# One core of an attention and feed-forward kernel: the last batch's residual chain placed otherwise among the plain units

## The reference, cut to what matters

```python
x = x + xattn(layernorm(x), ctx, mask, ...)         # 16 heads; the result is scaled and layer-normed
h = layernorm(x)
h = fwht(h * SU_ug) / 64                            # Walsh-Hadamard transform over 512 columns
h = silu(h @ W_gate.T * s_gate) * (h @ W_up.T * s_up)   # 2048 columns
h = fwht(h * SU_dp) / 64
x = x + h @ W_down.T * s_down
```

## Time and profile before

| what | value |
|---|---|
| median of 3 runs | 1454.08 us (1452.18 to 1454.42) |
| the profiled execution, its own time | 1452.16 us |
| its span, first to last instruction | 1450.3 us |
| mean granted TensorE clock | 0.997 of full speed |
| TensorE busy with products | 1407.1 us (97%) |
| VectorE busy | 1107.4 us (76%) |
| ScalarE busy | 814.2 us (56%) |
| GpSimd busy | 88.8 us (6%) |
| eight plain units, first product to the last before the pairs | 929.87 to about 1030 us |

### The profile page before, as it was taken

The page is one execution under the profiler, slowest core; times in us unless marked ns, Lnnn a source line. Parts: engine busy times, 40 slices in busy tenths (PEclk is TensorE's granted clock), DMA queues, the critical chain, the costliest instruction groups (busy, mean ns, idle before and its releaser), DMA issues. The chain is left out here.

```text
span 1450.3 us, 25099 instructions
## 1 busy us (share of the span) xinstructions
PE 1407.1 (97%) x10344; PEld 954.1 (66%) x10344; DVE 1107.4 (76%) x1655; ACT 814.2 (56%) x1018; POOL 88.8 (6%) x128
## 2 busy tenths in 40 slices
PE   7999999999999999999999999998999999999997
PEld 6787333788333688333689333586788888888886
DVE  6953999885999895899885899887866565656654
ACT  5345999535999635899635899534533333333330
POOL 1000000101000100000100000110010010000100
PEclk9999999999999999999999999999999999999999
DMA  8453000536100425000424500362345554454435
GB/s 275 151 185 153 9 10 10 177 104 218 52 10 10 147 98 190 21 17 10 141 74 175 241 17 10 97 240 86 146 147 208 189 182 149 163 208 176 174 145 174
DMA packets 54785, 180.91 MB, mean 125 GB/s; under 512 B 11168, under 2 KB 25760, under 8 KB 42384
## 3 DMA queue, kind: packets, MB, share of 16 engines
q1 hardware_dynamic: 39696, 116.08, 22.2%
q0 software_dynamic: 14976, 63.23, 12.7%
HBM read 111.97 MB, written 67.31 MB: 124 GB/s over the span
## 5 line engine op out<-in xcount | busy, mean ns | idle before, releaser
L960 ACT ACTIVATE cx_probs<-cx_sc,proj_mbias 128x1024 f32<-128x1024 f32 (+1 forms) x416 | 442.7, 1113 | 48.2 <-PE cx_sc L1234 24.6
L1103 DVE TENSOR_SCALAR cx_probs<-cx_probs 128x1024 f32<-128x1024 f32 (+1 forms) x416 | 269.8, 685 | 50.8 <-ACT cx_probs L960 49.0
L1069 DVE TENSOR_TENSOR cx_padd<-cx_probs,cx_probs 128x1024 f32<-128x1024 f32 x192 | 234.0, 1219 | 0.9
L1234 PEld LDWEIGHTS cx_sc<-cx_q,cx_kt 32*128 32x128 f32 (+1 forms) x2496 | 103.7, 180 | 192.2 <-ACT cx_probs L960 172.5
L1257 PE MATMUL cx_acc<-cx_probs,cx_vt 128*32 128x512 f32 (+1 forms) x1664 | 218.1, 596 | 3.8 <-DVE cx_probs L1103 3.8
L1234 PE MATMUL cx_sc<-cx_q,cx_kt 32*128 32x512 f32 (+1 forms) x2496 | 206.5, 425 | 10.2 <-ACT cx_probs L960 7.1
L140 PE MATMUL ff_yp<-hand_wds,ff_held 128*128 128x512 f32 x624 | 143.7, 389 | 0.1
L1702 DVE TENSOR_TENSOR ff_x<-ff_yp,ff_x 128x512 f32<-128x512 f32 x128 | 85.4, 688 | 68.5 <-PE ff_yp L140 57.6
L140 PEld LDWEIGHTS ff_yp<-hand_wds,ff_held 128*128 128x128 f32 x624 | 117.0, 188 | 24.8 <-DVE ff_kept L1765 0.5
L1269 PE MATMUL cx_tot<-cx_padd,cx_ones 128*32 128x256 f32 x1536 | 120.8, 390 | 0.0
L902 ACT ACTIVATE cx_kt<-cx_sc,proj_bk 128x256 fp32r<-128x256 f32 (+1 forms) x96 | 44.5, 478 | 74.6 <-PE cx_sc L140 74.2
(11 more groups left out here) (294 smaller groups left out, 2057.7 us busy)
## 6 DMA issues: line engine op xcount, KB each, us to landing
ff_x<-scr_x SPq DMA_DIRECT2D x32, 1024.0 KB, 5.0
scr_x<-ff_x SPq DMA_DIRECT2D x28, 1024.0 KB, 4.7
proj_raw<-in_ctxT SPq DMA_DIRECT2D x20, 512.0 KB, 5.7
hand_wds<-scr_wd POOLq DMA_DIRECT2D x7, 1024.0 KB, 9.9
scr_q<-cx_q SPq DMA_DIRECT2D x3, 2048.0 KB, 6.5
cx_wo<-scr_wo POOLq DMA_DIRECT2D x3, 2048.0 KB, 13.7
scr_xs<-cx_xs POOLq DMA_DIRECT2D x3, 2048.0 KB, 7.9
cx_q<-scr_q SPq DMA_DIRECT2D x3, 1536.0 KB, 10.8
```

What stands on the lines that cost most here:

```text
L960: nc.scalar.activation(prob(N)[0:r], bank_of(n)[0:r], ACT.Exp, bias=mbias[0:r, b, t:t + 1], scale=SCALE).then_inc(exp_done, 1)
L1069: nc.vector.tensor_tensor(padd[z][(g * QP + j) % 2][:], prob(2 * i + z)[:], prob(2 * i + 2 + z)[:], ALU.add).then_inc(added[z], 1)
L1103: nc.vector.tensor_scalar(prob(N)[0:r], prob(N)[0:r], LOW, HIGH, ALU.max, ALU.min).then_inc(clip_done, 1)
L1234: last = nc.tensor.matmul(bank_of(2 * i + h // 2)[0:r, h % 2], kt[own, z, c, t * P:t * P + r], q[own, y, c], start=n == 0, stop=n == 2)
```

## The change

Five edits. ScalarE does the second root (k = 1) behind the silu of unit 4 instead of at the end of unit 3, and VectorE does `normed`, and a turned sum with it, ahead of unit 4's low part instead of behind it. TensorE does transposes 0 and 1 between the up and the gate product of unit 5, and 2 and 3 between the halves of its gate product; ScalarE's signs and VectorE's butterfly go ahead of unit 5's silu and `hf`. The rotation goes ahead of `down(5)`; its high and low parts are done in two halves with other high and low parts between. The two turned sums (k = 6, 7) go from unit 3 to the end of unit 5, and the second `sums.add` and its neighbours move behind the rotation. The residual sum of the last batch takes the tiles in the order 2, 3, 0, 1, and two waits of `products` on it are lowered to fit.

```diff
--- before.py
+++ after.py
@@ -284,8 +284,8 @@
             act.wait_ge(self.fly, b * 2 + 1 + c // 2)
             nc.scalar.activation(r.fs[:, 0, c], r.xR[:, c], ACT.Copy).then_inc(self.fly_hi, 1)
 
-    def rotated_hi(self, nc, act, r, b):
-        for c in range(HC):
+    def rotated_hi(self, nc, act, r, b, chunks=range(HC)):
+        for c in chunks:
             act.wait_ge(self.rot_done, b * HC + c + 1)
             if c == 0 and b < B - 1:
                 act.wait_ge(self.x1_stored, b * 16 + 16)
@@ -378,8 +378,8 @@
             dve.wait_ge(self.fly_hi, b * (HC + 2) + c + 3)
             nc.vector.tensor_tensor(r.fs[:, 1, c], r.xR[:, c], r.fs[:, 0, c].bitcast(F32), ALU.subtract).then_inc(self.fly_lo, 1)
 
-    def rotated_lo(self, nc, dve, r, b):
-        for c in range(HC):
+    def rotated_lo(self, nc, dve, r, b, chunks=range(HC)):
+        for c in chunks:
             dve.wait_ge(self.xs_hi, b * HC + c + 1)
             nc.vector.tensor_tensor(r.xs[:, 1, c], r.bank(c), r.xs[:, 0, c].bitcast(F32), ALU.subtract).then_inc(self.xs_lo, 1)
 
@@ -1619,12 +1619,10 @@
                         turned[0].split_hi(nc, act, 1)
                     elif u == 2:
                         chain.root(nc, act, LAST, 0)
-                    elif u == 3:
-                        chain.root(nc, act, LAST, 1)
                     elif u == 5:
-                        chain.signs(nc, act, room, LAST)
+                        chain.rotated_hi(nc, act, room, LAST, range(2))
                         sums.split_hi(nc, act, 1, 1)
-                        chain.rotated_hi(nc, act, room, LAST)
+                        chain.rotated_hi(nc, act, room, LAST, range(2, HC))
                         act.wait_ge(last_out, 16)
                         act.wait_ge(chain.xn_done, B * ST)
                         for n in Turned.SPLIT[1:]:
@@ -1632,9 +1630,13 @@
                         sums.split_hi(nc, act, 1, 0)
 
                 def unit(u):
+                    if u == 5:
+                        chain.signs(nc, act, room, LAST)
                     act.wait_ge(gate_done, u + 1)
                     at_least(act, hf_done, u - 1)
                     nc.scalar.activation(silu[u % 2][:], gp[buffer(u)][:], ACT.Silu, scale=scale[:, 1, u % GC:u % GC + 1]).then_inc(silu_done, 1)
+                    if u == 4:
+                        chain.root(nc, act, LAST, 1)
                     act.wait_ge(hf_done, u + 1)
                     at_least(act, down_done, u - 1)
                     nc.scalar.activation(hs[u % 2][:, 0], hf[u % 2][:], ACT.Copy).then_inc(h_hi, 1)
@@ -1693,7 +1695,7 @@
                     if s < B:
                         dve.wait_ge(down_done, (s + 1) * GC)
                     dve.wait_ge(x1_in[b % 2], (1 + sum(x % 2 == b % 2 for x in BATCHES[:s])) * 16)
-                    for j in range(ST):
+                    for j in (2, 3, 0, 1) if s == LAST else range(ST):
                         bank = yp[j]
                         if s >= B:
                             k = (s - B) % 2 * ST + j
@@ -1719,37 +1721,39 @@
                     elif u == 3:
                         chain.residual_sum(nc, dve, room, LAST)
                         chain.residual_moments(nc, dve, room, LAST)
-                        dve.wait_ge(gate_done, 2 * GC)
-                        for k in range(6, 8):
-                            turned[0].add(nc, dve, k)
                     elif u == 4:
                         chain.normed(nc, dve, room, LAST)
                         dve.wait_ge(xs_in[2], 16)
                         turned[1].add(nc, dve, 0)
                     elif u == 5:
                         sums.add(nc, dve, 1, 1)
-                        chain.butterfly(nc, dve, room, LAST)
+                        chain.rotated_lo(nc, dve, room, LAST, range(2))
                         turned[0].split_lo(nc, dve, 1)
+                        chain.rotated_lo(nc, dve, room, LAST, range(2, HC))
                         sums.add(nc, dve, 1, 0)
-                        chain.rotated_lo(nc, dve, room, LAST)
                         sums.split_lo(nc, dve, 1, 1)
+                        dve.wait_ge(gate_done, 2 * GC)
+                        for k in range(6, 8):
+                            turned[0].add(nc, dve, k)
                         for n in Turned.SPLIT[1:]:
                             turned[0].split_lo(nc, dve, n)
 
                 def unit(u):
                     if u == 0:
                         beside(0)
+                    if u == 5:
+                        chain.butterfly(nc, dve, room, LAST)
                     dve.wait_ge(silu_done, u + 1)
                     at_least(dve, h_hi, u - 1)
                     nc.vector.scalar_tensor_tensor(hf[u % 2][:], up[buffer(u)][:], scale[:, 0, u % GC:u % GC + 1],
                                                    silu[u % 2][:], ALU.mult, ALU.mult).then_inc(hf_done, 1)
+                    if u == 4:
+                        beside(u)
                     dve.wait_ge(h_hi, u + 1)
                     nc.vector.tensor_tensor(hs[u % 2][:, 1], hf[u % 2][:], hs[u % 2][:, 0].bitcast(F32), ALU.subtract).then_inc(h_lo, 1)
                     if u == 0:
                         for k in range(2, 6):
                             turned[0].add(nc, dve, k)
-                    if u == 4:
-                        beside(u)
                     if u % GC == 0 and u:
                         accumulate(u // GC - 1)
                     if u and u != 4:
@@ -1851,10 +1855,16 @@
                     if u == 0:
                         pe.wait_ge(hand.ug_in, 16)
                     at_least(pe, hf_done, u if 2 < u < UN - 1 else u - 1)
-                    for w, acc in ((0, up), (1, gp)):
-                        last = split_product(nc, acc[buffer(u)][:], lambda t, c: ugs[:, w, t, c, i * P:(i + 1) * P],
-                                             lambda t, c: xs[b][:, t, c])
-                    last.then_inc(gate_done, 1)
+                    own = slice(i * P, (i + 1) * P)
+                    split_product(nc, up[buffer(u)][:], lambda t, c: ugs[:, 0, t, c, own], lambda t, c: xs[b][:, t, c])
+                    if u == 5:
+                        chain.transposes(nc, pe, room, LAST, range(2))
+                    split_product(nc, gp[buffer(u)][:], lambda t, c: ugs[:, 1, t, c, own], lambda t, c: xs[b][:, t, c],
+                                  chunks=2)
+                    if u == 5:
+                        chain.transposes(nc, pe, room, LAST, range(2, HC))
+                    split_product(nc, gp[buffer(u)][:], lambda t, c: ugs[:, 1, t, c + 2, own], lambda t, c: xs[b][:, t, c + 2],
+                                  chunks=2, first=False, resumed=True).then_inc(gate_done, 1)
 
                 def down(u):
                     b, i = u // GC, u % GC
@@ -1882,9 +1892,9 @@
                             else:
                                 pe.wait_ge(hf_done, UN - 1)
                         if product == 5 and w == 0:
-                            pe.wait_ge(y_read, rows(n - 1, 6 if n else 7) if n < SU - 1 else rows(n - 2, 6))
+                            pe.wait_ge(y_read, rows(n - 1, 6 if n else 5) if n < SU - 1 else rows(n - 2, 6))
                         if product == 2 and w == 0 and n == 0:
-                            pe.wait_ge(y_read, B * ST)
+                            pe.wait_ge(y_read, B * ST - 2)
                         if product == 2 and w and n == 0:
                             pe.wait_ge(hf_done, UN)
                         if product in (5, 6, 7, 4) and n < PAIRS and w:
@@ -1924,11 +1934,9 @@
                 gate_up(4)
                 down(3)
                 gate_up(5)
-                chain.transposes(nc, pe, room, LAST, range(2))
                 down(4)
-                chain.transposes(nc, pe, room, LAST, range(2, HC))
+                chain.rotation(nc, pe, room, LAST)
                 down(5)
-                chain.rotation(nc, pe, room, LAST)
                 gate_up(6)
                 gate_up(7)
                 down(6)
```

## The result

| | median | profiled execution | span |
|---|---|---|---|
| before | 1453.88 us (9 runs) | 1452.16 us | 1450.3 us |
| changed | 1449.66 us (9 runs) | 1449.66 us | 1447.8 us |

The ratio of changed to before is 0.9973, 95% interval 0.9962 to 0.9984: about 4 us faster (2.3 to 5.5 by the interval), where 3.8 were forecast. One of the nine runs of the changed kernel was a slow one of 4846.86 us; without it the median is 1449.41 us.

The account below looks back on a forecast made before the run. TensorE was taken as the bound, with halts of about 6.6 us in this stage. A gain of 3.37 us up to down(7) plus 0.42 from the tile order made 3.8 us: 1450.3 us, range 1447.7 to 1452.7.

Parts of the forecast that it names:

- the new halt: TensorE before down(6): a new wait of 1.8 us, released by the residual sum, as a sign of the forecast.
- Root behind the fifth gate: Start of the sixth unit: silu and hf come earlier, so TensorE is not held; 1.49 + 0.14 us saved.
- Transposes inside the sixth unit: Between the sixth unit's products: transposes start at about 981.8, 0.1 us lost to their held weight load.
- Rotation ahead of down(5): After down(4): rotation starts without a wait, loses 0.4 us before its third bank; seventh unit starts 5.0 us earlier.
- What is late next: Before the seventh hf: 9.4 us of VectorE work, tied with ScalarE, delays down(6); 1.8 of 5.0 us lost, 3.37 stay.
- Turned sums later, order of tiles: Second upper product: its 0.91 us halt goes, only 0.42 passes the later copy, where the wait grows to about 0.7.
- The rule on table loads: ScalarE table switches: the skill page adds a drain of about 1380 ns to each load, giving 1.4 us gain, not 3.8.
- Rival (a): ScalarE's moved table switches: each load stands twice its 1.28 us; gain only 1.5 us, 1452.6; chance 10%.
- (b): Down(6) is not held, VectorE's block being shorter or hf going ahead of it; gain 5.4 us, 1448.7; chance 8%.
- (c): Halts only move to the seventh silu and down(6), VectorE setting the pace; under 2 us left, around 1453.5; chance 11%.
- (d): Sixth unit: xn comes late inside it and holds TensorE; slower, 7.2 us against 3.8, 1457.5; chance 5%.

## Why the prediction was right

By the lengths the stage gained 4.00 us where 3.79 were forecast: 5.14 against 5.0 at unit 7, 3.60 against 3.37 at down(6). The path, the new halt and what holds it were as forecast. That the medians lie 4.2 us apart and not 3.8 is within their scatter and says nothing more.

**Root behind the fifth gate.** Right, by its steps: silu right behind its gate, hf without the sums in front, unit 6 at 2.72 behind down(3), root 1.29 after the load's start, no load for the Copy. Put back, it costs 1.54 us (67.69 against 66.15).

**Transposes inside the sixth unit.** Forecast to lose 0.1 us to xn; the row at 983.10 follows the up product at its usual distance, so nearly nothing was lost. Put behind the unit they cost 1.88 us, and the signs come 1.87 later. xn ended at 983.03, 0.07 us before the transposes: it was in time with almost nothing to spare.

**Rotation ahead of down(5).** Forecast to lose 0.4 us before its third bank; it lost 0.28: 1.04 between 992.95, the second product of the bank before, and 993.99, and 0.96 from there to the next, where 0.86 is usual. The difference of 0.12 is the larger part of the 0.15 us by which unit 7 was earlier than forecast. Put back, it costs 4.0 us, more than any other edit.

**What is late next.** This term decided whether the forecast was near 5.4 or 3.8, and it held: VectorE's row was forecast at 9.4 us and took 9.33 (998.96 to 1008.29), the start of down(6) was forecast 1.82 behind the end of unit 7's issue and came 1.74 behind it (1008.41 + 2.72 to 1012.87; the row's 1.58 counts from the end of the last result). Of the 5.0 us, 1.8 off leave 3.2 and not 3.37; the 0.2 between them are the longer product behind the old halt (1003.97 to 1006.82, 2.85 for 2.72) and 0.07 ahead of 1015.05, which the sum carries without naming them. That VectorE and ScalarE tie there was in the sum, and the versions that relieve one of them show it: neither alone helps, both do.

**Turned sums later, order of tiles.** Forecast 0.42 for the order; 0.39 measured by putting it back. The place of the rest was forecast only in part: the wait at the copy was to grow to 0.7 and is 0.43, and some 0.2 stand at 1036.26 instead, a wait that the prediction does not have. The turned sums' own worth was not given a number of its own in the prediction; it is nothing (66.08 against 66.15), since their 2.4 us stand in VectorE's row instead.

**The rule on table loads.** Three switches can be read (before: 977.59 to 978.88; after: 978.57 to 979.86 and 987.32 to 988.61), each 1.29 us from the start of the load to the start of the next activation. The drain of about 1380 ns that the Trainium skill, ScalarE: Activation LUTs, "What ACT_TABLE_LOAD costs", adds is in none of them, though the input of the load's next activation was there in each case (after: the input of the root at 978.73, the gate product at 987.81; before: the gate product at 976.40). Nor does anything stand ahead of the loads: each starts 0.02 to 0.03 us behind the end of the activation before. Rival (a) falls with it.

**The other rivals.** (b) fails by the row 1012.87. (c) had the halts only move: of the 5.14 us won at unit 7, 1.54 were lost again at down(6), and the other 3.60 stayed. (d) fails by 983.10: xn was there in time.

The edits put back one at a time cost 1.54, 1.88, 4.0, 0.39 and 0 us, 7.8 together, while the whole change is worth 4.0. The orders on the engines were made to fit each other, so the worth of one edit taken from the whole is not its share of the gain. Not every part was put back alone: no run has the signs and the butterfly behind silu and hf again, `normed` behind the low part, or the second `sums.add` ahead of the rotation.

## What to carry to other kernels

Price an edit by the chain that runs across engines to the next hard wait, and not by the halt it removes: work moved off one engine's path stands in another row of work, and if a later wait hangs on that row, the halt moves there. Where two engines arrive together, relief of one shows nothing; test the pair before calling the wait unmovable. When differences are a few tenths of a percent, compare lengths between two fixed products inside a profile; they repeated within 0.04 us here, while the medians of the same kernel differed by 0.5. Look at the granted clock between the two products first: the one length that did not repeat (71.66 and 70.15) had a fall of the clock in it.

## What the runs showed of the hardware

The granted clock falls to half for a few microseconds, at places that differ between executions. One fall in the profile of before, in a stretch of 2 us:

```profile
586.00:588.00 2.00, 2.00 (x16) 0.25 (x12) 1.69 (x3) 1.57 (x3) 0.00 (x0) 0.50 0.00 0
```

Stretches of 20 us ahead of the stage, in the profiles of before, of the changed kernel, and of the version with the transposes behind the unit:

```profile
580.00:600.00 20.00, 17.60 (x169) 6.73 (x167) 15.02 (x20) 16.47 (x17) 0.00 (x0) 0.91 0.13 39
```

```profile
360.00:380.00 20.00, 17.59 (x166) 7.07 (x167) 14.07 (x19) 15.52 (x16) 0.00 (x0) 0.91 0.36 144
```

```profile
60.00:80.00 20.00, 20.00 (x90) 16.72 (x89) 12.18 (x31) 4.45 (x8) 0.00 (x0) 0.89 0.23 87
140.00:160.00 20.00, 17.80 (x148) 7.12 (x146) 12.92 (x17) 14.21 (x15) 0.00 (x0) 0.83 0.13 41
```

Before has 0.91 at 580 to 600 where the changed kernel has 1.00, and the other way round at 360 to 380. The changed kernel's second profile has 0.91 at 360 and also at 800, where the first has 1.00, so the places differ for one and the same kernel too. The version with the transposes behind has 0.94, 0.89 and 0.83 at 40, 60 and 140 and two more stretches at 0.91 later; its profile reached down(3) 6.9 us later than the changed kernel's, with a span of 1456.0, while its median is 1451.6. It is the latest of the fourteen profiles and the one with the most time at the lower clock; the second in both (981.12, clock 0.94, 0.89, 0.91 and 0.91 in four stretches) is that with ScalarE's high part moved. But the falls are not the whole of it: eight profiles have one stretch of 0.91 each and still reach down(3) between 975.74 and 978.25, before and the changed kernel among them. What makes these 2.5 us is open.

A halt of 2.6 us before down(6) was followed by a fall in one profile of two; halts of 1.6 us there were followed by none in seven profiles. Whether a halt makes a fall likelier, so that removing it is worth more than its length now and then, is not shown.
